# A second attention layer begun among the last expert units of a fused two-layer transformer kernel

## The reference, cut to what matters

```
x = x + L0_xattn(layernorm(x), ctx)     # quantised attention, 16 heads
x = x + L0_ffn(layernorm(x))            # 32 experts, top 8 with rerouting, silu(g) * u
x = x + L1_xattn(layernorm(x), ctx, ids)
x = x + L1_ffn(layernorm(x))            # int32 weights, 256 -> 704 -> 256

def L1_xattn(q, kv, seg_id):            # 16 heads, 128 plus 64 rotary
    kv_c, q_c = kv @ W_kvc, q @ W_dq
    q_nope = heads(q_c @ W_uq);  q_rope = rope(heads(q_c @ W_qr))
    k_nope = heads(kv_c @ W_uk); k_rope = rope(kv_c @ W_kr)
    scores = (q_nope . k_nope + q_rope . k_rope) / sqrt(192)
    good = (k_ids <= seg_id) & (k_ids >= seg_id - 8)
    attn = softmax(where(good, scores, -1e30))
    return (attn @ heads(kv_c @ W_uv)) @ W_o
```

## Time and profile before

| what | us |
|---|---|
| median of 3 runs | 845.04 |
| lowest and highest run | 843.58, 847.16 |
| span of the profiled execution | 841.8 |
| PE busy, share of the span | 782.3, 93% |
| DVE, ACT, POOL busy | 663.8, 535.0, 469.1 |

### The profile page before, as it was taken

How to read it: one execution, slowest core, us unless ns; L and a number is a source line. 1 busy time by engine, 2 the same in 40 slices (tenths; PEclk the granted TensorE clock), 3 DMA queues, 4 the chain that set the end, 5 groups by cost and what they waited for, 6 DMA issues and landing times.

```text
span 841.8 us, 14343 instructions
## 1 busy us (share of the span) xinstructions
PE 782.3 (93%) x4848; PEld 670.3 (80%) x4848; DVE 663.8 (79%) x1563; ACT 535.0 (64%) x1236; POOL 469.1 (56%) x786
## 2 busy tenths in 40 slices
PE   3687999999999999999899999999999999798998
PEld 2566788888888888888788878998888877577787
DVE  7789899899998989979889794865654589976634
ACT  6788877787778877788664555433332268974332
POOL 3688969779686895858855676442210015980000
PEclk9699999999999999999999999999999999999999
DMA  7000120011200121000200323967421010100001
GB/s 242 14 0 1 39 76 1 2 39 39 76 1 1 39 66 48 2 2 1 68 26 14 127 64 98 243 167 249 133 63 51 1 45 14 51 14 0 1 1 51
DMA packets 28265, 45.59 MB, mean 54 GB/s; under 512 B 3937, under 2 KB 18081, under 8 KB 28065
## 3 DMA queue, kind: packets, MB, share of 16 engines
q1 hardware_dynamic: 26800, 41.31, 17.0%
q10 hardware_dynamic: 1392, 3.37, 1.1%
HBM read 43.49 MB, written 1.18 MB: 53 GB/s over the span
## 4 chain that ended last, share of the span: by engine, by line
PE 59%; DVE 22%; ACT 11%; issue 5%; DMA 2%; POOL 1%; SPq 1%; ACTq 0%; DVEq 0%
PE PS L772 16%; PE PS L842 8%; PE PS L632 6%; PE PS L727 4%; PE PS L701 4%; PE PS L663 4%; PE PS L953 2%; PE PS L684 2%; PE PS L654 2%; PE PS L673 2%; DVE st L1638 2%; DVE yb L1540 2%; ACT P L1111 1%; PE PS L711 1%; DMA l_KM<-share 1%
## 5 line engine op out<-in xcount | busy, mean ns | idle before, releaser
L2222 POOL TENSOR_SCALAR raw<-raw,mvq,rsq 128x128 f32<-128x128 f32 x312 | 182.9, 600 | 1.6
L772 PE MATMUL PS<-xq,WH 128*128 128x512 f32 x472 | 148.5, 396 | 1.0 <-ACT l_x2T L997 1.0
L772 PEld LDWEIGHTS PS<-xq,WH 128*128 128x128 f32 x472 | 86.3, 190 | 18.1 <-issue 2.1
L632 PE MATMUL PS<-WH,xq 128*128 128x256 f32 (+1 forms) x256 | 88.7, 366 | 8.1 <-DVE xq L1544 8.1
L772 PE MATMUL PS<-xq,WL 128*128 128x512 f32 x236 | 92.5, 392 | 0.0
L632 PE MATMUL PS<-WL,xq 128*128 128x256 f32 (+1 forms) x256 | 84.5, 349 | 0.0
L1111 ACT ACTIVATE P<-PS,sm 128x256 f32<-128x256 f32 x128 | 61.0, 497 | 25.7 <-DVE sm L1702 25.6
L842 PE MATMUL PS<-xq,m_hh 128*128 128x256 f32 x384 | 69.9, 283 | 2.5 <-DVE m_hl L1998 1.2
L1638 DVE BATCH_NORM_STATS2 st<-raw 128x6 f32<-128x128 f32 x320 | 70.6, 277 | 1.5 <-ACT raw L1083 1.5
L701 PE MATMUL PS<-PT,vr 128*128 128x256 f32 x256 | 66.5, 382 | 4.7 <-ACT PT L997 4.7
L663 PE MATMUL PS<-kT,qT 128*128 128x256 f32 x256 | 65.9, 380 | 1.8 <-ACT qT L1100 1.8
(11 more groups left out here) (301 smaller groups left out, 2177.7 us busy)
## 6 DMA issues: line engine op xcount, KB each, us to landing
wst<-in_wgu SPq DMA_DIRECT2D x24, 256.0 KB, 4.0
l_KM<-share SPq DMA_DIRECT2D x16, 384.0 KB, 3.9
wst<-in_wall SPq DMA_DIRECT2D x18, 256.0 KB, 3.1
l_KM<-share SPq DMA_DIRECT2D x16, 256.0 KB, 5.2
dst<-in_wdn SPq DMA_DIRECT2D x24, 128.0 KB, 3.4
wst<-in_wkvx SPq DMA_DIRECT2D x8, 256.0 KB, 3.3
l_KM<-share SPq DMA_DIRECT2D x16, 128.0 KB, 4.4
m_pre<-in_wo ACTq DMA_DIRECT2D x1, 2048.0 KB, 10.2
```

What stands on the lines that cost most here:

```text
L632: t = e.matmul(PS[:, b, o:o + n], xq[s][:, k, c * 128:(c + 1) * 128], W[:, k, w0:w0 + n], start=(k == 0 and i == 0), stop=(k == 1 and i == 1))
L772: t = e.matmul(PS[:, b, :], W[wi][:, gu, k, :], a[:, k, cols], start=(n == 0), stop=(n == 5))
L2222: t = e.tensor_scalar(v, v, mvq[:, par, n, 0:1], rsq[:, par, n:n + 1], ALU.add, ALU.mult)
```

## The change

1. The last units of `MOE` are ordered 20 to 23 of half 0, then 20 to 23 of half 1; before, 21 to 23.
2. `outmix` and `keymix` are cut into quarters. Behind the down product of the last unit but one, PE now does outmix 0, turn 0 and 1, outmix 1, compress 0 and 1, the last down product, queries (0, 0), outmix 2 and 3, keymix 0 and 1, queries (0, 1), keymix 2 and 3; then in `late_order` queries (1, 0), turn 2 and 3, scores 0, queries (1, 1), compress 2 and 3. ACT's copies follow this order.
3. DVE: settle(0) advances by 13 steps per unit; the mask (`find_mask`) is made at unit (20, 0); settle(1) is cut after ten steps for `turn_q(0, 0)`.
4. POOL makes the sine products of 14 of the 16 units; DVE keeps those in `SINE_D`. POOL's add now also waits for DVE's cosine product.
5. The buffers that are used early lie beside `msg`, `mhh`, `mhl` (with a pad of 336 floats), `PT1`, `S1` and `S2` behind them. Units 0 to 2 of the rotation use S[2], S[1], S[0]; unit 3 and later use `m_pre`.
6. Every kind of bank of the second attention has fixed banks (`home`): lt and qc their batch's number (in the experts' part 4 and 5), qr 6 and 7 (4 and 5), scores 0 and 1 or 4 and 5 by turns, lp 2 and 3, lv 2 to 5.
7. POOL makes the weight pieces 0 and 1 before the second attention; SP issues seg and fsc earlier.
8. At the end, project 2 stands before turn_p 7 on PE, and the add of batch 1 before the scaling of chunk 7 on DVE.

```diff
-MOE = [(j, h) for j in range(21) for h in range(2)] + [(j, h) for h in range(2) for j in range(21, 24)]
+MOE = [(j, h) for j in range(20) for h in range(2)] + [(j, h) for h in range(2) for j in range(20, 24)]
...
-    for n in range(2, len(MOE) + 2):
-        if n < len(MOE) and MOE[n][0] >= NPRE:
+    for n in range(2, len(MOE)):
+        if MOE[n][0] >= NPRE:
             do("gate_up", *MOE[n])
-        if n == len(MOE):
-            do("outmix")
-        if n >= 2:
-            do("down", *MOE[n - 2])
-    do("keymix")
-QUERIES = {0: (3,), 1: (4,), 2: (5,), 3: (6,), 4: (7,)}
-FPIECES = ((0,), (1, 2), (3, 4), (5,), (6, 7, 8))
+        do("down", *MOE[n - 2])
+    do("down", *MOE[-2])
+    do("outmix", 0)
+    do("turn", 0)
+    do("turn", 1)
+    do("outmix", 1)
+    do("compress", 0)
+    do("compress", 1)
+    do("down", *MOE[-1])
+    do("queries", 0, 0)
+    do("outmix", 2)
+    do("outmix", 3)
+    do("keymix", 0)
+    do("keymix", 1)
+    do("queries", 0, 1)
+    do("keymix", 2)
+    do("keymix", 3)
+QUERIES = {1: (4,), 2: (5,), 3: (6,), 4: (7,)}
+FPIECES = ((), (2,), (3,), (4,), (5, 6, 7, 8))
+SINE_D = ((0, 0), (0, 2))
 def late_order(do):
-    for a, b in ((0, 1), (2, 3)):
-        do("turn", a)
-        do("turn", b)
-        if a:
-            do("queries", 1, 0)
-        do("compress", a)
-        do("compress", b)
-        if a == 0:
-            do("queries", 0, 0)
-            do("queries", 0, 1)
+    do("queries", 1, 0)
+    do("turn", 2)
+    do("turn", 3)
     for n in range(12):
         if n < 8:
             do("scores", n)
+        if n == 0:
+            do("queries", 1, 1)
+            do("compress", 2)
+            do("compress", 3)
...
-        if 1 < n < 10:
+        if 1 < n < 9:
             do("turn_p", n - 2)
...
+        if n == 9:
+            do("turn_p", 7)
...
+            "lt": lambda bb: bb, "qc": lambda bb: bb, "qr": lambda bb, u: 6 + u % 2, "lo": lambda bb: 7,
+            "ft": lambda bb: 6 + (bb == 3), "ls": lambda c, z: 4 * (c % 2) + z, "lp": lambda c, z: 2 + z,
+            "lv": lambda bb, z: 2 + z, "fg": lambda j, h: 2 * (FFN.index((j, h)) % 2),
...
 # ACT, swap_q: the wait for the buffer
-                    if n > 3:
-                        w.wait_ge(added.sem, added.at[units_q[n - 2 if n > 5 else n - 4]])
+                    if n > 4:
+                        w.wait_ge(added.sem, added.at[units_q[n - 2]])
 # ACT, the order of the copies
+            take_bp(0)
+            take_lt(0)
+            take_lt(1)
+            take_bp(1)
+            take_qc(0)
+            take_qc(1)
+            swap_q(0, 0)
+            take_bp(2)
+            take_bp(3)
+            take_km(0)
+            take_km(1)
+            swap_q(0, 1)
+            take_km(2)
+            take_km(3)
+            swap_q(1, 0)
+            take_lt(2)
+            take_lt(3)
...
+                if n == 0:
+                    swap_q(1, 1)
                 if n < 8:
                     exps2(n)
+                if n == 0:
+                    take_qc(2)
+                    take_qc(3)
 # DVE
-                    for _ in range(12):
+                    for _ in range(13):
                         next(settling, None)
+                if n == MOE.index((20, 0)):
+                    find_mask()
             weave(settling)
-            weave(settle(1))
+            settling = settle(1)
+            for _ in range(10):
+                next(settling)
+            turn_q(0, 0)
+            weave(settling)
+            turn_q(0, 1)
+            turn_q(1, 0)
...
+                if n == 8:
+                    add_l(1)
                 if 0 < n < 9:
                     scale(n - 1)
 # POOL, add_q
-                    w.wait_ge(turned_q.sem, turned_q.at[bb, u])
+                    if (bb, u) in SINE_D:
+                        w.wait_ge(turned_q.sem, turned_q.at[bb, u])
+                    else:
+                        v = tqs[n].rearrange("p (a t) -> p a t", a=2)
+                        w.wait_ge(swapped.sem, swapped.at[bb, u])
+                        e.tensor_tensor(v, v, tb_[:, 256:512].unsqueeze(1).to_broadcast([128, 2, 256]),
+                                        ALU.mult).then_inc(po.sem, 1)
+                        w.wait_ge(po.sem, po.up())
+                    w.emptied(("qr", bb, u))
```

More of the change, by code:

```diff
@@ L440, in program @@
             "gate_up": lambda j, h: [("g", j, h), ("u", j, h)],
-            "outmix": lambda: [("bp", z) for z in range(4)], "keymix": lambda: [("km", z) for z in range(8)]}), (0, 1, 2, 3))
+            "outmix": lambda z: [("bp", z)], "keymix": lambda y: [("km", 2 * y), ("km", 2 * y + 1)]}), (0, 1, 2, 3))
         B.ring(fills(moe_order, {
@@ L515, in program @@
         swapped = count("swapped", [(bb, u) for bb in range(4) for u in range(4)])
-        turned_q = count("turned_q", [(bb, u) for bb in range(4) for u in range(4)])
+        turned_q = count("turned_q", SINE_D)
         gated_5 = count("gated_5", range(2))
@@ L881, in tensor @@
-            experts = {"early": early, "xs": xs, "logits": logits, "absorb": absorb, "turn_oh": turn_oh, "rows": rows,
-                       "turn_cw": turn_cw, "gate_up": early, "down": down, "outmix": outmix, "keymix": keymix}
-            moe_order(lambda kind, *a: experts[kind](*a))
+                b = fill(("bp", z))
+                for o in range(2):
+                    for p in (2 * z, 2 * z + 1):
+                        h = 2 * p + (o ^ (z % 2))
+                        t = e.matmul(PS[64 * o:64 * o + 64, b, p % 2 * 256:p % 2 * 256 + 256], wuv[:, h, :],
+                                     wo[:, h, :], start=True, stop=True)
@@ new lines, in outmix, with keymix @@
+                t.then_inc(full[b], 1)
+            def keymix(y):
+                banks = [fill(("km", 2 * y + o)) for o in range(2)]
+                emptied(("aw", y))
+                for i in range(2):
+                    for o, b in enumerate(banks):
+                        rows = slice(64 * o, 64 * o + 64)
+                        t = e.matmul(PS[0:96, b, i * 256:(i + 1) * 256], AT[rows, 2 * y + i, :], KA[rows, :],
+                                     start=True, stop=True)
+                        if i:
+                            t.then_inc(full[b], 1)
@@ L906, in queries @@
                     t.then_inc(full[b], 1)
+            experts = {"early": early, "xs": xs, "logits": logits, "absorb": absorb, "turn_oh": turn_oh, "rows": rows,
+                       "turn_cw": turn_cw, "gate_up": early, "down": down, "outmix": outmix, "keymix": keymix,
+                       "turn": turn2, "compress": compress, "queries": queries}
+            moe_order(lambda kind, *a: experts[kind](*a))
             def scores2(c):
@@ L2107, in split_f @@
                                 xq[0][:, :, cols].bitcast(F32), ALU.subtract).then_inc(free[b], 1)
-            for part in range(3):
-                turn_q(part // 2, part % 2)
             def gate_f(n):
@@ L2482, in sync @@
             stage_share(20)
+            w.filled(("aw", 3))
+            e.dma_start(seg[:], A["seg"]).then_inc(seg_in, 16)
+            e.dma_start(fsc[:], A["fsc"]).then_inc(fsc_in, 16)
             stage_dn(22)
```

159 lines of the change are left out of this document (66 added, 93 removed).

## The result

The changed kernel takes 854.37 us (median of 4 runs, 852.22 to 855.96), the kernel before 844.77 us beside it: a ratio of 1.0105, 95% interval 1.0079 to 1.0131, slower by 9.6 us. A second set of 6 runs gave 1.0094, 1.0077 to 1.011. The forecast was 847.0 us and its range ended at 851.5, so the loss lies outside it. The profiled execution's span is 853.8 us for 841.8.

The account below looks back on a forecast made before the run. DVE, with ACT right behind, was taken to bound the late stages. +3.4 us up to the first output projection, −2.35 in the tail and 0.8 for low clock, taken as +1.9 on 845.04, gave 847.0 us; range 839.5 to 851.5.

Parts of the forecast that it names:

- PE's waits up to `project(0)`: From the last expert units to the first output projection: `project(0)` starts at 743.1 for 739.7, +3.4 us.
- the tail: End of the late stage: `project(2)` first, starting at 768.6 for 771.0; feed-forward at 779.0 for 781.35, gain 2.35 us.
- the clock: PE at half clock after new waits in the late stage: 0 to 1.6 us each, 0.8 us taken in all.
- The first norm moves, and PE loses its cover: `settle(0)` in units 45 and 46: PE waits 3.5 us from 672.5 for unit 46's split, formerly covered by `outmix`.
- The second norm meets GpSimd: `settle(1)` after `turn_q(0, 0)`: GpSimd's instructions block DVE's small steps; norm ends about 695.3, 3.1 us later than alone.
- no lock: Second norm: small steps slip between GpSimd's instructions, norm ends at 692.3, total 843.8 us; chance 0.15 shared with no new wait.
- The chain to the first exponentials: GpSimd's sine and add in series between ACT's swaps: table load for the exponentials at 707.3, before at 703.36.
- The steady part: Iterations after the table load: ACT becomes the bound, 37.2 us to chunk 4's exponentials ending at 744.5; before 740.9.
- What is free: Mask in unit 40, weight pieces 0 and 1 early, earlier SP issues, pad and separate buffers: no cost.
- The text's own fallback: Mask and early pieces: if the covering idle times were gone, the mask would cost its 2.5 us of DVE.
- three new waits: New PE waits in the late stage: 3.5 us at 672.5, 4.0 at 709 and 3.1 at 732.
- slower: the low clock: PE at half clock after waits at 672.5 and 732: two spells 849.3 us, three 850.9; chance 0.24 with longer chain.

Follow-up runs that it names:

- cover, mask and copies mended: Changed kernel with outmix 0 to 2 before unit 46's down product, mask two units earlier, all sine products on DVE, compressed-query copies before the first exponentials: 842.86 us, ratio 0.9974.
- the pieces spread too: Changed kernel with those same four edits, and GpSimd's weight pieces 2 and 3 moved before the second loop step, 7 and 8 alone last: 840.97 us, ratio 0.9950.
- the single repairs: Changed kernel, one edit each: outmix before down product 848.46 us; pieces early 850.46; compressed queries first 850.38; DVE sines for batches 2, 3 848.57, for 0, 1 849.04.

## Why the prediction was wrong, step by step

Term by term, the prediction against the first profile:

| term | predicted us | measured us |
|---|---|---|
| PE's waits up to `project(0)` | +3.4 | +2.63 |
| the tail, PE's waits from there to the feed-forward | −2.35 | +0.49 |
| low clock, both stages | +0.8 | +4.5 |
| the mask | 0 | +1.55 |

The first term held. The other three are the steps that failed, the clock and the tail above all. The rest of the 12.0 us is mostly the 3.07 of chance ahead of unit 40.

*The first norm moves, and PE loses its cover*: right. The wait is 3.19 us for 3.5. What it was worth was not: 5.2 us with what hangs on it.

*The second norm meets GpSimd*: right in mechanism and size. The prediction had the norm end 6.8 us behind `turn_q(0, 0)`; it was 6.5, from 693.4 to 699.9, for an estimated 3.7 alone. The rule cited from the Trainium skill (SBUF — State Buffer, Who interferes with whom) held where it speaks: the product of two SBUF inputs at 695.77 took 1.13 us, until POOL's add had ended, and the next, with POOL idle, 0.16. The trace goes beyond that rule as the prediction gives it: the steps of 0.95 and 1.20 us are TENSOR_SCALAR steps with one tile as input, and were held too. The rival "no lock" is refuted.

*The chain to the first exponentials*: right. ACT waits 4.16 + 1.38 us for about 5; the table load, taken back by 4.62 us, is at 706.8 for 707.3.

*The steady part*: right about ACT in the changed kernel, once the clock is set apart. From the table load to the end of chunk 4's exponentials ACT takes 39.0 us for 37.2; it waits 2.8 us for 0.7, nearly all of it for queries that PE does late at half clock, and from 724 to 748 it is busy 23.3 of 24 us. `project(0)` came 4.5 us late in the stage's own time for 3.4, but of these 1.9 are low clock and only 2.63 waiting. POOL's load was set too low, 7.9 us per iteration for 8.6 (739.21 to 747.85), since POOL is blocked as well (its add at 743.12 took 2.12 us). What the prediction did not see is how near POOL's loop of sine, add and swap is to the bound: in the old order it is the bound.

*What is free*: wrong twice. The mask cost 1.55 us here, since its cover, DVE's idle time, was crossed by GpSimd's pieces, which were priced at nothing. The prediction took GpSimd's idle time from the window 672.5 to 684, but the pieces ran from 647.6 to 654.1, beside the mask. The text's own fallback, 2.5 us, bounds it. It is the smaller fault, and in six of nine profiles it is not there.

*The tail*: wrong. A gain of 2.35 us was forecast; PE's waits grew by 0.49 instead, and with the low clock the stretch lost 3.07. The order alone gives about 1 us (on the kernel before). What took it is that POOL's pieces end 13.5 us later than before and the norm begins only 9.5 us later, so they meet, and the transposes of chunk 6 wait 3.49 us; and that the half clock then fell on `project(2)`, 8.72 us for 6.90. The prediction looked for POOL's lock in the second norm and did not ask where POOL's queue ends. Spreading the pieces gave 3.2 us back.

*The clock*: the term that was furthest off, 0.8 us for 4.5. The prediction took each spell as 3.4 us long. Its three new waits all came, somewhat shorter (3.19, 3.47 and 2.03 us for 3.5, 4.0 and 3.1), and a fourth, of 3.49 us in the tail, was not on its list. The two late spells were 6.8 us long, one of them in that fourth wait. Even with spells of 3.4 us the 0.8 was low: by the prediction's own count of one spell in three waits, and 1.6, 0.8 and 1.6 us for them, it comes to 1.3. The rival "slower: the low clock" came nearest, with 4.3 to 5.9 us.

In terms of edits: the sine products on GpSimd cost 7 to 9 us, shown in both directions (added alone, +8.7; taken out alone, −8.0), and the rest of the change is worth nothing that can be told. With cover, mask and copies mended it gains 0.3%, with the pieces spread too 0.5%; that a lost cover, the mask and the late copies eat what the order gives is the reading of these versions together, not a separate measurement. The cover and the pieces matter while GpSimd carries the sines; of the early copies that is less sure. How the 7 to 9 us divide between the chain, the blocked norms and the clock isn't settled: the single repairs (5.2, 3.2, 3.3, 5.1, 4.6) add up to 21 us, far more than the loss, so they can't act each on its own part. That each breaks the same string of waits at another link fits this, and is not shown.

## What to carry to other kernels

Before work is moved to an idle engine, follow that engine's queue to its end and ask what runs beside it there; the average share (POOL at 57%) says nothing of it, and POOL's stream held DVE's small steps, 0.17 us each, for up to 1.20 us. If a moved product stands between two steps of another engine's chain, price it as latency in that chain, not as load. Price a new PE wait at the wait and the low clock that can follow it: here 2.8 us less of waiting in one place went with 5.2 us.

## What was unexpected of the hardware

The granted clock fell to 0.50 for 6.8 us at a stretch in the late stage, beginning in waits of 3.47 and 3.49 us, where the kernel before showed 3.4 us after 2.37. The same wait of 3.2 us before unit 46 was followed by no spell, by 3.4 us and by 6.8 us in different profiles.

Code that no edit touches differed by up to 4.9 us at 634 us between profiles (−1.8 to +3.1 against the kernel before), and the records show 13.6 to 27.3 us of low clock ahead of that point. One profile of each kernel isn't enough to place a difference of 3 us.
